# Cross-attention with a routed FFN on one core: the step of TensorE over the routed blocks spans four blocks in place of three

## The reference

```python
x = x + cross_attention(layernorm(x), ctx)             # 4 x 512 tokens of 512, 16 heads
xt = layernorm(x).reshape(-1, 512)                     # 2048 tokens
gate = xt @ Wr + br                                    # 7 experts
_, ids = top_k(gate + gate_bias, 2)                    # each token goes to two experts
probs = softmax(gate kept only at ids)
u = einsum('nh,ehi->eni', xt, Wup) + bup
g = silu(einsum('eni,eij->enj', u, Wgate) + bgate) * u
eo = einsum('enj,ejh->enh', g, Wdown) + bdown
out = einsum('ne,enh->nh', probs, eo)
su = xt @ Wsu + bsu                                    # one shared expert, for all tokens
so = (silu(su @ Wsg + bsg) * su) @ Wsd + bsd
x = x + out + so
```

## Time and profile before

| what | value |
|---|---|
| median of 3 runs | 1005.14 us (1005.12 to 1009.39) |
| the profiled execution | 1006.48 us, span 1004.8 us |
| TensorE busy over the span | 910.4 us, 91% |
| VectorE, ScalarE, GpSimd busy | 646.0, 464.0, 621.5 us |
| stage of the routed blocks | 568.22 us (first turn of x) to 938.64 us |
| late stage | 938.64 us to the end |

### The profile page before, as it was taken

How to read it: one execution, slowest core, us unless ns; L and a number is a source line. 1 busy time by engine, 2 the same in 40 slices (tenths; PEclk the granted TensorE clock), 3 DMA queues, 4 the chain that set the end, 5 groups by cost and what they waited for, 6 DMA issues and landing times. The chain is left out here.

```text
span 1004.8 us, 16883 instructions
## 1 busy us (share of the span) xinstructions
PE 910.4 (91%) x5047; PEld 404.9 (40%) x5048; DVE 646.0 (64%) x1019; ACT 464.0 (46%) x846; POOL 621.5 (62%) x565
## 2 busy tenths in 40 slices
PE   3789895799999899989999599999999999999998
PEld 1345442122111222246644245555455545554443
DVE  7787776688888888357675144544554454544388
ACT  3376565788878887623352023223223323322440
POOL 6465555468767774543137488888999999300373
PEclk9989997699999999989999799999999999999999
DMA  7134634445445432134426745556556645435667
GB/s 243 63 100 116 184 109 148 138 172 177 168 164 183 142 104 66 43 106 146 168 95 247 246 149 197 183 186 178 196 163 202 204 163 199 144 121 189 226 194 236
DMA packets 106058, 162.26 MB, mean 161 GB/s; under 512 B 12536, under 2 KB 55608, under 8 KB 105616
## 3 DMA queue, kind: packets, MB, share of 16 engines
q1 hardware_dynamic: 93056, 116.38, 35.5%
q0 software_dynamic: 12896, 45.10, 13.7%
q10 hardware_dynamic: 48, 0.05, 0.0%
HBM read 107.88 MB, written 53.48 MB: 161 GB/s over the span
## 5 line engine op out<-in xcount | busy, mean ns | idle before, releaser
L1089 ACT ACTIVATE p_t<-a_psT 128x512 f32<-128x512 f32 x256 | 138.9, 595 | 46.9 <-PE a_psT L1212 45.6
L1136 DVE TENSOR_REDUCE nm<-quad 128x4 bf16<-128x1984 f32 x60 | 133.9, 2231 | 35.6 <-PE quad L1197 35.6
L1039 POOL TENSOR_TENSOR p_sum<-p_t,p_t 128x512 f32<-128x512 f32 x64 | 80.9, 1274 | 50.2 <-ACT p_t L1089 49.9
L1978 PE MATMUL e_psY<-w_exp,e_gT 128*128 x456 | 110.7, 379 | 0.9 <-ACT e_y L1919 0.9
L1978 PE MATMUL quad<-w_exp,e_xT 128*128 x456 | 107.0, 385 | 1.6 <-DVE e_xT L1933 1.6
L1978 PE MATMUL quad<-w_exp,e_uT 128*128 x456 | 106.3, 384 | 1.7 <-DVE e_uT L1933 1.7
L215 POOL TENSOR_TENSOR w_exp<-e_raw,w_exp 128x1024 f32 (+1 forms) x42 | 91.7, 2182 | 6.0 <-POOL e_raw L212 4.5
L1212 PE MATMUL a_psT<-q_stk,k_stk 98*128 98x512 f16 x256 | 84.3, 400 | 11.3 <-ACT p_t L1089 8.9
L207 POOL TENSOR_TENSOR w_exp<-e_raw,ws_tile 128x1024 f32 (+1 forms) x42 | 80.5, 1916 | 6.2 <-DMA e_raw<-in_L_ffn_Wup_dram 5.4
L1905 ACT ACTIVATE e_uT<-quad 128x512 f16<-128x512 f32 x38 | 22.7, 597 | 124.0 <-PE quad L1968 124.0
L1926 ACT ACTIVATE e_g<-e_g 128x512 f32<-128x512 f32 x38 | 23.9, 629 | 103.6 <-DVE e_g L1936 103.6
(11 more groups left out here) (340 smaller groups left out, 1812.7 us busy)
## 6 DMA issues: line engine op xcount, KB each, us to landing
xs_dram<-zero SPq DMA_DIRECT2D x38, 256.0 KB, 7.0
e_x<-xs_dram SPq DMA_DIRECT2D x38, 256.0 KB, 4.1
bias<-in_L_ffn_bup_dram SPq DMA_DIRECT2D x38, 256.0 KB, 3.8
bias<-in_L_ffn_bgate_dram SPq DMA_DIRECT2D x38, 256.0 KB, 3.7
ys_dram<-e_y SPq DMA_DIRECT2D x38, 256.0 KB, 3.8
q_dram<-q_st SPq DMA_DIRECT2D x24, 256.0 KB, 3.0
k_dram<-k_st SPq DMA_DIRECT2D x24, 256.0 KB, 3.6
q_stk<-q_dram SPq DMA_DIRECT2D x64, 96.0 KB
```

Source lines behind the costliest of these rows:

```text
L1039: pool.tensor_tensor(p_sum[:, w % SUMS, :], probs(w, 0), probs(w, 1), ALU.add).then_inc(s["sum_1"], 1)
L1089: act.activation(probs(w, k), psT[:, k % 2], ACT.Exp, scale=SCALE / (QS * QS)).then_inc(s["exp"], 1)
L1136: dve.tensor_reduce(nm[:, i, :, 0:1].rearrange("p h o -> p (h o)"), psS[:, :, 0:NMAIN], AX.X, ALU.max, negate=True)
L1978: ins = pe.matmul(dst[:, :], stationary, moving, start=(k == 0 and chunks[0] == 0), stop=(k == len(terms) - 1 and chunks[-1] == KD - 1))
```

## The change

TensorE's step spans blocks n+1 to n-3 in place of n+1 to n-2. It is now: turns of g(n-2), x(n+1) and u(n) in a row, the whole of down(n-3), up(n+1), gate(n). ScalarE, VectorE and SyncE have their parts in an order to match, and there is one step more at the end (N + 3 in place of N + 2). The two products of the late stage that TensorE did behind the last step stand in steps N and N + 1, and down of the last block is behind them. SyncE loads the bias row of the gate one step later than that of up, with a register load of its own.

```diff
 def step(n, j, i):                                   # TensorE
     if live(n, 2):
-        w2 = expert(n - 2, at - 2) - 1
-        pe.wait_ge(s["gT_l"], n - 1)
-        at_least(pe, s["y_r"], n - 2)
-        product(psY, gT[:, j], w2, 2, range(0, KD // 2))
+        pe.wait_ge(s["g_r"], n - 1)
+        at_least(pe, s["gT_l"], n - 2)
+        transposes(psGT, g, s["gT_t"])
+    if live(n, -1):
+        pe.wait_ge(x_ld[(j + 1) % 2], (i + 1 if j == 0 else i + 2) * 16)
+        at_least(pe, s["xT_l"], n + 1)
+        transposes(psX, x_in[:, (j + 1) % 2], s["xT_t"])
     if live(n, 0):
         pe.wait_ge(s["u_r"], n + 1)
         at_least(pe, s["uT_l"], n)
         transposes(psUT, u[:, j], s["uT_t"])
-    if live(n, 1):
-        pe.wait_ge(s["g_r"], n)
-        at_least(pe, s["gT_l"], n - 1)
-        transposes(psGT, g, s["gT_t"])
-    if live(n, 0):
-        w = expert(n, at) - 1
-    if live(n, 2):
-        product(psY, gT[:, j], w2, 2, range(KD // 2, KD)).then_inc(s["y_mm"], 1)
+    if live(n, 3):
+        w3 = expert(n - 3, at - 3) - 1
+        pe.wait_ge(s["gT_l"], n - 2)
+        at_least(pe, s["y_r"], n - 3)
+        product(psY, gT[:, (j + 1) % 2], w3, 2).then_inc(s["y_mm"], 1)
     if live(n, -1):
-        pe.wait_ge(x_ld[(j + 1) % 2], (i + 1 if j == 0 else i + 2) * 16)
-        at_least(pe, s["xT_l"], n + 1)
-        transposes(psX, x_in[:, (j + 1) % 2], s["xT_t"])
         after = expert(n + 1, at + 1)
-    if live(n, 0):
-        pe.wait_ge(s["uT_l"], n + 1)
-        at_least(pe, s["g_in"], n)
-        product(psG, uT, w, 1).then_inc(s["g_mm"], 1)
-    if live(n, -1):
         pe.wait_ge(g_["split_done"], after * (2 * NM) + 2 * NM + 1)
         pe.wait_ge(s["xT_l"], n + 2)
         at_least(pe, s["u_r"], n + 1)
         product(psU, xT[:, (j + 1) % 2], after - 1, 0).then_inc(s["u_mm"], 1)
+    if live(n, 0):
+        w = expert(n, at) - 1
+        pe.wait_ge(s["uT_l"], n + 1)
+        at_least(pe, s["g_in"], n)
+        product(psG, uT, w, 1).then_inc(s["g_mm"], 1)
+    if isinstance(n, int) and n == N:
+        pe.wait_ge(late_ld, 32)
+        pe.wait_ge(g_["split_done"], (E + 1) * (2 * NM) + 2 * NM + 1)
+        pe.wait_ge(s["xT_l"], N)
+    if isinstance(n, int) and N <= n < N + UP_EARLY:
+        late_up(n - N, (psX, psU)[n - N])
...
 def step(n, j, i):                                   # SyncE
     if not isinstance(n, int) or n + 2 < N:
         load(n + 2, j)
     if live(n, -1):
-        biases(n + 1)
-    if live(n, 2):
-        sp.wait_ge(s["y_r"], n - 1)
-        sp.dma_start(rows("ys_dram", n - 2), y[:, j]).then_inc(y_st[j], 16)
+        bias_row(n + 1, 0, "L0_ffn_bup", "b_up", "u_r")
+    if live(n, 0):
+        bias_row(n, 1, "L0_ffn_bgate", "b_gate", "g_in")
+    if live(n, 3):
+        sp.wait_ge(s["y_r"], n - 2)
+        sp.dma_start(rows("ys_dram", n - 3), y[:, (j + 1) % 2]).then_inc(y_st[(j + 1) % 2], 16)
...
 def step(n, j, i):                                   # VectorE, the new order
+    if live(n, 1):
+        dve.wait_ge(s["g_mm"], n)
+        dve.wait_ge(s["b_gate"], n * 16)
+        at_least(dve, s["gT_t"], n - 1)
+        biased(g[:, :], psG, 1, s["g_in"], n)
     if live(n, -1):
         dve.wait_ge(s["xT_h"], n + 2)
         lo_part(xT[:, (j + 1) % 2], psX).then_inc(s["xT_l"], 1)
...
```

More of the change, by code:

```diff
@@ L1825, in run @@
             step(n, n % 2, n // 2)
-        for n in range(N - 2, N + 2):
+        for n in range(N - 2, N + 3):
             step(n, n % 2, n // 2)
@@ L1843, in load, with bias_row @@
                 sp.dma_start(x_in[:, j], rows("xs_dram", n)).then_inc(x_ld[j], 16)
-            def biases(n):
+            def bias_row(n, m, name, done, used):
                 k = sp.value_load(blk_k[0:1, ds(n, 1)], min_val=1, max_val=E)
-                for m, (name, done, used) in enumerate((("L0_ffn_bup", "b_up", "u_r"), ("L0_ffn_bgate", "b_gate", "g_in"))):
-                    at_least(sp, s[used], n)
-                    sp.dma_start(bias[:, m, :], t[name][ds(k - 1, 1), :].rearrange("o n -> (o n)").partition_broadcast(P)).then_inc(s[done], 16)
+                at_least(sp, s[used], n)
+                sp.dma_start(bias[:, m, :], t[name][ds(k - 1, 1), :].rearrange("o n -> (o n)").partition_broadcast(P)).then_inc(s[done], 16)
             def step(n, j, i):
@@ L1865, in _ @@
             load(0, 0)
-            biases(0)
+            bias_row(0, 0, "L0_ffn_bup", "b_up", "u_r")
             load(1, 1)
@@ L1907, in step @@
             def step(n, j, i):
+                if live(n, -1):
+                    act.wait_ge(s["xT_t"], n + 2)
+                    at_least(act, s["u_mm"], n)
+                    hi_part(xT[:, (j + 1) % 2, 0], psX).then_inc(s["xT_h"], 1)
+                if live(n, 1):
+                    act.wait_ge(s["g_in"], n)
+                    act.activation(g[:, :], g[:, :], ACT.Silu).then_inc(s["silu"], 1)
                 if live(n, 0):
@@ L1911, in step @@
                     hi_part(uT[:, 0], psUT).then_inc(s["uT_h"], 1)
-                if live(n, 1):
-                    act.wait_ge(s["gT_t"], n)
-                    at_least(act, s["y_mm"], n - 2)
-                    hi_part(gT[:, (j + 1) % 2, 0], psGT).then_inc(s["gT_h"], 1)
                 if live(n, 2):
-                    act.wait_ge(s["y_mm"], n - 1)
-                    at_least(act, y_st[j], 16 * (i - 1))
-                    act.activation(y[:, j], psY[:, :], ACT.Copy, scale=1.0 / WS).then_inc(s["y_r"], 1)
-                if live(n, -1):
-                    act.wait_ge(s["xT_t"], n + 2)
-                    at_least(act, s["u_mm"], n)
-                    hi_part(xT[:, (j + 1) % 2, 0], psX).then_inc(s["xT_h"], 1)
-                if live(n, 0):
-                    act.wait_ge(s["g_in"], n + 1)
-                    act.activation(g[:, :], g[:, :], ACT.Silu).then_inc(s["silu"], 1)
+                    act.wait_ge(s["gT_t"], n - 1)
+                    at_least(act, s["y_mm"], n - 3)
+                    hi_part(gT[:, j, 0], psGT).then_inc(s["gT_h"], 1)
+                if live(n, 3):
+                    act.wait_ge(s["y_mm"], n - 2)
+                    at_least(act, y_st[(j + 1) % 2], 16 * (i - 2 + j))
+                    act.activation(y[:, (j + 1) % 2], psY[:, :], ACT.Copy, scale=1.0 / WS).then_inc(s["y_r"], 1)
             step(-1, 1, -1)
@@ L1954, in step @@
                 if live(n, 0):
[L1955 to L1960, removed]
+                    dve.wait_ge(s["uT_h"], n + 1)
+                    lo_part(uT, psUT).then_inc(s["uT_l"], 1)
+                if live(n, 2):
+                    dve.wait_ge(s["gT_h"], n - 1)
+                    lo_part(gT[:, j], psGT).then_inc(s["gT_l"], 1)
+                if live(n, 1):
+                    dve.wait_ge(s["silu"], n)
+                    dve.tensor_tensor(g[:, :], g[:, :], u[:, (j + 1) % 2], ALU.mult).then_inc(s["g_r"], 1)
+                if live(n, -1):
+                    dve.wait_ge(s["u_mm"], n + 2)
+                    dve.wait_ge(s["b_up"], (n + 2) * 16)
+                    at_least(dve, s["g_r"], n)
+                    at_least(dve, s["uT_t"], n)
+                    biased(u[:, (j + 1) % 2], psU, 0, s["u_r"], n)
             step(-1, 1, -1)
@@ L1969, in transposes, with product @@
                 ins.then_inc(done, 1)
-            def product(dst, a, w, m, chunks=range(KD)):
+            def product(dst, a, w, m):
                 terms = []
-                for c in chunks:
+                for c in range(KD):
                     for x, part in ((0, 0), (1, 0), (0, 1)):
@@ L1977, in product, with late_up @@
                 for k, (stationary, moving) in enumerate(terms):
-                    ins = pe.matmul(dst[:, :], stationary, moving, start=(k == 0 and chunks[0] == 0),
-                                    stop=(k == len(terms) - 1 and chunks[-1] == KD - 1))
-                return ins
+                    ins = pe.matmul(dst[:, :], stationary, moving, start=(k == 0), stop=(k == len(terms) - 1))
+                return ins
+            def late_up(c, dst):
+                terms = [(q, x, y) for q in range(KD) for x, y in ((0, 0), (1, 0), (0, 1))]
+                for i, (q, x, y) in enumerate(terms):
+                    ins = pe.matmul(dst[:, :], w_exp[:, q // 2, 0, y, q % 2, c * P:(c + 1) * P], g_["xT_late"][:, 0, q, x, :],
+                                    start=(i == 0), stop=(i == len(terms) - 1))
+                ins.then_inc(g_["late_u_mm"], 1)
             expert_of = {}
@@ L2031, in _ @@
             expert_of.clear()
-            for n in range(PEELED + rounds * UNROLL, N + 2):
+            for n in range(PEELED + rounds * UNROLL, N + 3):
                 step(n, n, n // 2)
[L2035 to L2044, removed]
 def late(nc, t, sem, g_, out):
```

16 lines of the change are left out of this document (2 added, 14 removed).

## The result

The changed kernel takes 997.35 us (median of 6 runs, 995.83 to 999.43) against 1005.13 (6 runs, 1004.6 to 1009.39). The ratio is 0.9919, with a 95% interval of 0.9902 to 0.9935: 7.8 us or 0.8% faster. The forecast was 1000.4 with a range of 997.0 to 1004.0, so the time is at the lower edge of the range, and beyond the half per cent on which faster and same were divided. Same, with 0.49, was what I gave the most, and it was wrong.

The account below looks back on a forecast made before the run. TensorE was taken to bound the routed stage, losing time to waits for u. Steady steps -6.0, head -0.9, tail +0.9 and clock +1.4 gave -4.6 us from 1005.14, so 1000.5, stated as 1000.4, range 997.0 to 1004.0.

Parts of the forecast that it names:

- What bounds the stage, and why u is late: Routed stage: TensorE bounds it; VectorE's product g x u, lengthened by GpSimd up to 2.2 us, delays u.
- -6.0 in the steady steps: Steady routed steps: TensorE's waits for u go, hidden by a down, up and gate; -6.0 us.
- the 1.2 at the heads of the rounds: Hardware loop's round heads: 8 steps longer by 0.14 to 0.17 us, 1.2 together, left standing in the sum.
- The head, -0.9 of 0 to -1.8: Start of the routed stage: idle time even, clock dip stays (0) or goes (-1.8 us); -0.9 taken.
- The tail, +0.9: Last gate to the late stage: 14.3 us against 13.43, as the last y has no cover; +0.9 us.
- The clock behind the gap, +1.4 out of 0 to +2.6: Start of the late stage: clock may fall behind a 3.4 to 3.5 us idle gap; +1.4 us taken.
- Rivals 2 and 3: 2: u still waits behind VectorE's product, 1006 to 1008.5, chance 0.04; 3: lower clock through the head, 1018, chance 0.03.
- rival 4: Round-head losses vanish as well and no clock dip at either end; 996.5 to 998 us, chance 0.1.
- The first (up waits for x's lo): Steady steps: up(n+1) waits for x's lo, 0.15 to 0.2 us each; 1004 to 1007 us, chance 0.09.

Follow-up runs that it names:

- silu_in_psum: Kernel before the change, with silu writing to the gate's PSUM bank so the product g x u has one SBUF input; 999.33 us, ratio 0.9924.
- whole_down: Kernel before the change, with down(n-2) done uncut ahead of the turns and no block more in the step; 1027.11 us, ratio 1.021.
- slack_before: Kernel before the change, with two more VectorE instructions of 0.69 us ahead of each g; 1039.06 us, ratio 1.0333.
- slack_after: Changed kernel with two more VectorE instructions of 0.69 us ahead of each g; 1004.04 us, ratio 0.9976.
- before: The kernel before the change, unedited; 1005.13 us.
- before_again: The kernel before the change run once more, unchanged; 1005.37 us, ratio 1.0013.
- round8: Kernel before the change with hardware-loop rounds of eight steps in place of four; 1002.69 us in one run.
- tail_undone: Changed kernel with both late products again behind the last step, as before the change; 997.12 us, ratio 0.9915.
- four_late: Changed kernel with four late products done early, two where the change has them and two behind the last down; 999.95 us, ratio 0.9938.
- one_behind: Changed kernel with the second late product behind the last down in place of ahead of it; 995.31 us, ratio 0.9897; again 997.23 us.
- after: The changed kernel in its first measurement; 997.35 us, ratio 0.9919.
- after_third: The changed kernel once more, unchanged, on the same chip as a repeat with the second late product behind the last down; 998.19 us, ratio 0.9925.

## Why the prediction was wrong

By its own steps:

- **What bounds the stage, and why u is late: right.** silu_in_psum shows the cause, whole_down and slack_before what hangs on it.
- **-6.0 in the steady steps: right in kind, too small.** It was 7.15 us (315.87 less 34 x 9.08) by the profile I had, because the 1.2 at the heads of the rounds went as well; I had put that at the far end of the range and left it out of the sum. (The 1.2 is eight times 0.15: in my rows six of the eight heads read 0.14 to 0.17, and those of x(9) and x(17), 9.37 and 10.56, have more in them.) And my profile was the mild one: in the two others of this order, 8.5 and 8.7 us are lost, 8.1 on the mean of the three. That the heads cost nothing in the new order is seen in all eight profiles with it. Why is open. It is not the wait for u: in silu_in_psum that is gone, and all eight heads still cost 0.14 to 0.16. The change moved the load of the expert's number at the round's head as well, from ahead of the first half down to behind the three turns, and no run moves that alone.
- **The head, -0.9 of 0 to -1.8: the frame was wrong.** I took the clock's dip as a term of its own. Three profiles of the old order have 370.33 to 370.55 us for the stage, one with the dip and two without, since where it is missing another collision comes in step 3. A dip and a collision changed places there; I had one trace and added the one to the other as though they were independent. By my accounts the term measures -2.55 in my first two profiles (the stage's 9.01 us less, of which 7.15 are the steady steps and -0.7 the tail): gate(0) is 1.7 shorter without the dip, and up(0), which no edit touched, happened to be 0.8 shorter. On the means of three profiles of each order it is -1.2. The idle times were near what I had worked out: 0.35 and 0.58 in step 0 (0.3 and 0.9 foretold), 1.15 each in steps 1 and 2 (1.2 each).
- **The tail, +0.9: 0.7.** 17.15 us from the last gate in place of 13.43, less 3.03. The gap was 3.16, with 3.4 to 3.5 foretold.
- **The clock behind the gap, +1.4 out of 0 to +2.6: 1.4 on the mean.** It fell behind the gap of 3.15 to 3.16 us in each of the three profiles of the changed kernel, and in that of slack_after, where the late stage takes 69.04 us, 2.6 more than 66.4. So what I took from the Trainium skill, "TensorE: Matmul & The Clock Gate", section "Why this matters for your kernels", that the clock falls behind such a gap, agrees with four profiles of four; the price was 1.3 to 1.5 us in three of them and 2.6, about the 2.5 of the earlier trace rows, in the fourth. That I took the middle of the two bounds and met it is luck: the fall was no matter of half a chance here.

The sum of the measured parts: the stage, 370.45 on the mean of before, before_again and round8, is 361.83 in the three profiles of the changed kernel, 8.6 us less; the late stage, 66.4 against 67.8, 1.4 more. That is 7.2 us less, against 7.8 by the times, within their interval. The forecast had 6.0 against 8.6 for the stage (-6.0 - 0.9 + 0.9). **The failed step is the size of the steady term**, -6.0 against a measured -7.15 in the same profile and -8.1 on the mean: of the 2.6 us by which the stage gained more, 2.1 are this term, and 0.3 the head. It decided on which side of half a per cent the time fell: I set it by the collisions of one execution, and kept the 1.2 at the heads with no reason given for their outliving the change.

Rivals 2 and 3 did not come. Of rival 4 (996.5 to 998) the time came, and the heads vanished as it said, but not its other condition: the clock did fall at the far end. The first (up waits for x's lo) is right where there is no down: 1.15 us in steps 1 and 2, which was in the sum. What I did not see at all is the last gate's bias: it lands 6.0 us after its issue, with the two loads of the late stage under way, and g(37) is held by it:

```profile
911.07 0.69 DVE L1937 SCALAR_TENSOR_TENSOR e_g<-quad,bias 128x512 f32<-128x512 f32 x1 [3.23 <-DMA bias<-in_L_ffn_bgate_dram]
```

It costs the change nothing, since a down and a late product stand ahead of the turn of g(37), but it is what tail_undone paid with.

What differs ahead of the stage is chance: "start" is between 563.85 and 569.44 in fourteen profiles, in both orders. In my first two traces it was 3.1 us apart, all of it in stages that no edit touched. So the 10.6 us between the spans of these two are not what the change is worth.

## What to carry to other kernels

First see whether the collision can be taken away: one input of the product in PSUM (silu_in_psum) gave almost the whole gain with three lines. Where a short instruction of one engine now and then waits for a long one of another, count the distance to whoever needs its result in terms of the longest case, and lengthen that distance by work of other blocks; making down whole without the longer distance (whole_down) only moved the wait. Ask of every loss that you leave standing what would keep it alive in the new order. At a stage's end put work that needs nothing of the stage behind the last result, not ahead of it, but only as much as covers the store: in four_late what was taken out of the next stage was missing there. (By the profiles' parts one_behind is the best of the four endings, 2.3 to 3.1 us ahead of the changed kernel; the times side by side do not tell the two apart.)

## What was unexpected of the hardware

A dip of TensorE's clock does not simply add its price: in the old order the executions with and without it took the same time for the stage, within 0.25 us. Nor does the length of the last gap alone tell whether the clock falls: a gap of 3.00 us did no harm, one of 3.16 was followed by a fall in each of four profiles, and in slack_after the clock fell behind gaps of 1.87 and 1.97 us in two steps running. And kernels that are the same ahead of the routed stage differ there by up to 5.6 us from profile to profile. One such dip, at 419 us (granted clock 0.72 from 418 to 424 us in before_again, 1.00 in the profiles of after and after_third), is worth 1.7 us of it; this is an estimate from the share of the 6 us at the lower level.
